# Second expert layer in two parts of two sequences, the first part's routing moved into the end of the attention

## The chip, the cores and the metric

The kernel runs on one core of a Trainium2 chip. The metric is the device time of one execution in microseconds (us). In the rows the engines are PE (TensorE; PEld is its weight load), DVE (VectorE), ACT (ScalarE), POOL (GpSimd) and SP (SyncE); SPq is a transfer issued by SP. TensorE is granted one of two clocks, 1.2 GHz (0.50 in the rows) or 2.4 GHz (1.00).

## What is computed

Two layers over 4 sequences of 512 tokens with 128 features. Layer 0 is a state-space mixer and a mixture of eight experts with a shared one. Layer 1 is a causal attention with 16 heads of 8 features, and then the mixture that the change is about: each token goes to one of eight experts, and the expert's output is weighted with the softmax of the two largest logits and a gate.

```python
logits = flat @ Wr                                  # 2048 tokens x 8 experts
top_vals, top_idx = jax.lax.top_k(logits, 2)
w_top1 = jax.nn.softmax(top_vals, axis=-1)[:, 0]
h = gelu(flat @ W1[top1]); y = h @ W2[top1]         # 128 -> 512 -> 128, the chosen expert alone
x = x + gb * (w_top1 * y)
```

## The kernel before

Each engine runs its own list of instructions in order and waits on semaphores. The order in each list is written out by hand.

**Attention.** The loop `for it in range(-2, 17)` has one step `it` for each group of four heads of a sequence (16 groups), with eight slots `i`. In a slot PE does scores for the group two steps ahead (L1641, into a ring of three PSUM banks), transposed scores (`scores_T`, L1667 and L1672), and in every second slot the product with the values (L1686). DVE takes the maxima (L1221) and ACT the exponentials (L778). POOL cuts the maxima in three bf16 parts (`max_parts`, L522 to L528). PE transposes those (`maxima_T`, L1651), ACT copies them (L817), and SP writes them as rows beside the queries (L364); `scores_T` of the next step waits for these rows. Maxima for group 15 are taken at `it` 13, so DVE has next to nothing from there on.

**Router input.** `x3` of a sequence is ready after its four groups (`attn_out`, L1710 and L1243). `router_input` is a LayerNorm with shift and scale in five steps: statistics and moments on DVE (L387, L392), `ln_rstd` on POOL (L399, L401), normalise (L406), multiply (L539 or L1201), add (L544 or L1206). POOL does the last three for sequences 0 to 2, one half of a sequence's work at each step from `it` 10 on; DVE does them for sequence 3 after the loop.

**Routing, after the attention.** `router` transposes all four sequences (L1367), ACT copies them to SBUF (L831), and PE makes logits for 16 tiles of 128 tokens (L1509). DVE picks the largest (L1088 to L1092), PE counts ranks (L1750, L1751), and DVE turns these into a slot for every token, `posu` (L1275 to L1288). Slots are grouped in blocks of 128, each of one expert: at most 16 + 7 = 23 blocks (`NBLK`). POOL writes the rows of the 16 tiles to their slots in DRAM (`slots_x`, L586), and SP reads all slots back in four groups (L370).

**Blocks.** For each block j, PE transposes it (L1762) and DVE copies the result (L1321); DVE copies the expert's W1 into one of two buffers (L1319); PE makes the hidden layer (L1771, eight records), ACT applies the Gelu (L838), PE makes the output (L1782), and DVE copies it out (L1325). PE issues the transpose of block i+1, the hidden layer of block i and the output of block i-1 in turn. DVE also makes one tile of gate weights a block (L1329). POOL returns each block's rows to their tokens in DRAM (`tokens_y`, L592). After all 23 have landed SP reads four sequences back (L373), `combine` weights and adds them (L413, L415; POOL takes sequence 0, DVE the others), and SP stores them (L381).

## Time and profile before

| what | value |
|---|---|
| median of 3 runs | 581.68 us (579.49 to 581.73) |
| the profiled execution's own time | 577.07 us |
| its span | 575.2 us |
| busy: PE, DVE, ACT, POOL | 452.4, 392.0, 278.1, 271.6 us |
| mean granted clock of PE | 0.889 |

The span runs from the first to the last instruction; 1.87 us of the profiled execution lie around it. Busy time is a sum over stages with different limits. The stretch that the change touches is the last 135 us: the end of the attention (to 467.6 us), routing and row stores (to 511.1 us), blocks (to 558.5 us), and the return (to 575.2 us).

### The profile page before, as it was taken

To read this page: it belongs to the slowest core of one execution; us is meant where nothing else is said; L and a number is where in the kernel's file an instruction comes from. 1 tells how busy PE (TensorE), PEld (TensorE's weight loads), DVE (VectorE), ACT (ScalarE), POOL (GpSimd) and SP (SyncE) were. 2 spreads that over 40 slices of the span, in tenths; PEclk is the share of its full clock that TensorE was granted. 3 is DMA by queue.
4 is the path that set the end of the run, shared out by engine and by line. 5 is a ranking of instruction groups with operands and counts; after the bars stand their busy time and mean duration, and the time that the engine had idled before them with its cause. 6 is when DMAs were issued, how large, how long until landed. Compare 5 with 4: busy or idle time off the path is not lost.

```text
span 575.2 us, 10088 instructions
## 1 busy us (share of the span) xinstructions
PE 452.4 (79%) x3120; PEld 274.4 (48%) x3120; DVE 392.0 (68%) x1264; ACT 278.1 (48%) x518; POOL 271.6 (47%) x392
## 2 busy tenths in 40 slices
PE   3688778987998999994558998999999863059970
PEld 3545456766653444442323434435445343049970
DVE  5789738988655888886679687888898235025533
ACT  1568796653453544441223577678777831013220
POOL 4210038998301786664641047476655502714541
PEclk9988889999799999997775799999999985559995
DMA  8600000000335333310386012222300000141114
GB/s 354 169 1 1 0 2 2 1 2 1 144 148 125 99 106 99 107 62 2 108 208 124 4 31 88 82 86 85 84 5 4 3 0 10 52 123 36 36 38 146
DMA packets 25739, 39.94 MB, mean 69 GB/s; under 512 B 3228, under 2 KB 17756, under 8 KB 25164
## 3 DMA queue, kind: packets, MB, share of 16 engines
q1 hardware_dynamic: 21752, 30.42, 17.8%
q0 software_dynamic: 3936, 8.89, 5.2%
q8 instruction: 26, 0.43, 0.3%
q14 instruction: 25, 0.20, 0.1%
HBM read 27.55 MB, written 11.55 MB: 68 GB/s over the span
## 4 chain that ended last, share of the span: by engine, by line
PE 49%; DVE 18%; POOL 11%; issue 8%; ACT 6%; DMA 6%; SPq 0%; DVEq 0%; POOLq 0%; ACTq 0%
PE ps L1579 5%; PE ps L1581 5%; PE ps L1568 5%; PE ps L1686 4%; PE ps L1599 3%; PE ps L1771 3%; PE ps L1782 3%; POOL slots_x L586 3%; DVE rows L406 3%; PE ps L1391 2%; DVE moe L1221 2%; PE ps L1641 2%; POOL qk_parts L305 2%; DVE st L387 2%; PE ps L1672 2%
## 5 line engine op out<-in xcount | busy, mean ns | idle before, releaser
L1221 DVE CUSTOM_DVE_ANT_0 moe<-ps,const 128x512 bf16<-128x512 f32 (+3 forms) x256 | 110.5, 486 | 9.7 <-PE ps L1641 9.4
L778 ACT ACTIVATE arena<-ps 128x256 f32<-128x256 f32 (+3 forms) x128 | 85.8, 701 | 33.6 <-PE ps L1672 32.9
L476 POOL TENSOR_TENSOR arena<-arena 128x512 f32<-128x512 f32 x32 | 51.7, 1616 | 51.9 <-DVE arena L1139 51.7
L1641 PE MATMUL ps<-arena 48*128 48x128 bf16 (+3 forms) x256 | 56.1, 329 | 10.7 <-DVE arena L1221 4.7
L1672 PE MATMUL ps<-arena 51*128 51x128 bf16 (+3 forms) x256 | 52.2, 307 | 0.0
L1686 PE MATMUL ps<-arena 128*32 128x512 f32 (+3 forms) x512 | 48.4, 450 | 0.9 <-ACT arena L778 0.6
L1667 PE MATMUL ps<-bconst 64*128 64x64 bf16 x512 | 45.6, 195 | 1.2 <-ACT arena L778 0.5
L1641 PEld LDWEIGHTS ps<-arena 48*128 48x128 bf16 x256 | 16.7, 97 | 55.7 <-DVE arena L1221 31.7
L751 ACT ACTIVATE arena<-arena 128x512 f32<-128x512 f32 x32 | 20.2, 630 | 41.9 <-DVE arena L1139 41.6
L838 ACT ACTIVATE arena<-ps 128x512 f32<-128x512 f32 x23 | 13.7, 597 | 55.0 <-PE ps L1771 55.0
L592 POOL DMA_INDIRECT tokens_y<-arena,token_at x23 | 22.1, 960 | 32.5 <-DVE arena L1325 31.3
L950 DVE SCALAR_TENSOR_TENSOR arena<-ps,mixw,arena 128x511 f32<-128x511 f32 (+2 forms) x48 | 33.1, 737 | 5.2 <-ACT arena L643 5.2
L1667 PEld LDWEIGHTS ps<-bconst 64*128 64x128 bf16 x512 | 29.5, 97 | 12.0 <-ACT arena L778 4.5
L1579 PE MATMUL ps<-arena,moe 128*128 128x512 f32 x64 | 32.8, 593 | 1.8 <-DVE arena L1122 1.8
L441 POOL TENSOR_TENSOR arena<-arena 128x256 f32<-128x256 f32 x16 | 12.4, 776 | 44.4 <-DVE arena L933 40.5
L1581 PE MATMUL ps<-arena,moe 128*128 128x512 f32 x64 | 32.7, 592 | 0.0
L1568 PE MATMUL ps<-arena,moe 128*128 128x512 f32 x64 | 32.5, 592 | 0.0
L1130 DVE SCALAR_TENSOR_TENSOR arena<-ps,moe,arena 128x512 f32<-128x512 f32 x32 | 24.0, 751 | 12.3 <-PE ps L1581 12.2
L1762 PE MATMUL ps<-const,arena 128*128 128x128 f32 x23 | 6.5, 293 | 29.1 <-DMA arena<-slots_x 29.1
L1367 PE MATMUL ps<-const,rows 128*128 128x128 f32 x64 | 13.8, 367 | 17.6 <-DVE rows L406 14.9
L1771 PE MATMUL ps<-arena 128*128 128x128 f32 x184 | 26.5, 290 | 0.6 <-DVE arena L1321 0.5
L1139 DVE SCALAR_TENSOR_TENSOR arena<-ps,moe,arena 128x512 f32<-128x512 f32 x32 | 24.0, 751 | 3.5
(239 smaller groups left out, 1113.2 us busy)
## 6 DMA issues: line engine op xcount, KB each, us to landing
arena<-expert_weights SPq DMA_DIRECT2D x32, 256.0 KB, 3.2
arena<-moe_in SPq DMA_DIRECT2D x1, 4100.0 KB, 12.8
qk_parts<-arena SPq DMA_DIRECT2D x24, 128.0 KB, 2.3
qk_parts<-arena POOLq DMA_DIRECT2D x24, 128.0 KB, 2.3
arena<-qk_parts POOLq DMA_DIRECT2D x32, 96.0 KB, 2.5
arena<-qk_parts SPq DMA_DIRECT2D x8, 288.0 KB, 5.6
moe<-moe_in SPq DMA_DIRECT2D x1, 1936.0 KB, 13.8
slots_x<-zeros SPq DMA_DIRECT2D x1, 1518.0 KB, 19.6
```

The source lines that it names most:

```text
L476: pool.tensor_tensor(yacc[:, ts], yacc[:, ts], pr[:, i % 2, :], ALU.add).then_inc(sem("yacc"), 1)
L778: act.activation(pt[:, u % 4, :, 0:n], ps[:, 4 + 2 * k:6 + 2 * k, 0:n], ACT.Exp, scale=ATT_SCALE).then_inc(sem("probs"), 1)
L950: v.scalar_tensor_tensor(out=acc[b % 2][:, c, s:S], in0=ps[:, c, 0:S - s], scalar=w["conv_w"][:, 4 * c + 3 - s:4 * c + 4 - s], in1=acc[b % ...
L1221: v.tensor_tensor_reduce(out=junk[:, done % 2, 0:n], in0=ps[:, k, col:col + n], in1=w["mask"][:, (3 - qt) * P:4 * P], scale=1.0, scalar=3 ...
L1568: pe.matmul(ps[:, 6 + i % 2, :], w["w2"][:, e * D:(e + 1) * D], gT[:, i % 2, :], start=True, stop=True).then_inc(sem("p2_ps"), 1)
L1579: pe.matmul(ps[:, 2 + i % 2, :], w["w1"][:, e * D:(e + 1) * D], xm[:, i % 2, :], start=True, stop=True).then_inc(sem("p1_ps"), 1)
L1581: pe.matmul(ps[:, 4 + i % 2, :], w["w3"][:, e * D:(e + 1) * D], xm[:, i % 2, :], start=True, stop=True).then_inc(sem("p3_ps"), 1)
L1641: mm = pe.matmul(ps[:, k, col:col + n], qaug[lo:lo + KR, b % 2, 2 * g + j // 2, qt * P:(qt + 1) * P], kaug[lo:lo + KR, b % 2, 2 * g + j // ...
L1667: pe.matmul(ps[:, bank, HALF * qh:HALF * (qh + 1)], w["causal"][lo:lo + HALF, qh * P:(qh + 1) * P], w["half"][lo:lo + HALF, :], start=(qh ...
L1672: mm = pe.matmul(ps[:, bank, 0:n], kaug[lo:lo + KM, b % 2, 2 * g + jp, kt * P:(kt + 1) * P], qaug[lo:lo + KM, b % 2, 2 * g + jp, kt * P:S] ...
L1686: mm = pe.matmul(ps[32 * j:32 * j + 32, 3, kt * P:S], va[:, b % 2, kt, 4 * (s % QG) + j, :], pt[:, (2 * m + j // 2) % 4, j % 2, 0:n], star ...
L1771: mm = pe.matmul(ps[:, j % 2, q * P:(q + 1) * P], w1[:, j % 2, q * P:(q + 1) * P], xT[:, j % 2, :], start=True, stop=True)
```

## The change

The 16 tiles are two parts of 8 (sequences 0 and 1, sequences 2 and 3), each with slots and blocks of its own: 8 + 7 = 15 blocks a part, 30 in all.

- POOL's `router_input` of sequences 0 to 2 stands at other steps (it 10 to 14).
- At (13, 7), (14, 1), (14, 4) and (14, 6) PE transposes sequences 0 and 1, makes the logits of 8 tiles, and the ranks, in the ring's banks. ACT copies the two transposes at (14, 0) and (14, 2). DVE does `choose(0)` at (14, 5), and blocks, positions, experts and second best of part 0 at (14, 7).
- POOL then writes part 0's eight tiles (`to_slots(0)`), and only behind them does `ln_rstd` of sequence 3. It returns three blocks of part 0, writes part 1's tiles, and returns the rest; `combine` of sequences 0 and 1 runs on POOL after blocks 4 and 7 of part 1.
- SP reads part 0's slots in three groups once its rows have landed, then part 1's.
- Sequence 2's transpose stands between PE's last two transposes of the attention. After `attn_out(3)` PE has the transpose of sequence 3, two block transposes, part 1's logits, block 0, and on. DVE does the routing of part 1 in pieces between the steps of blocks 0 to 4.
- The last combine is sequence 3 on DVE and sequence 2 on POOL.
- Loads of the constants share one semaphore, and the blocks' buffers lie in areas of the attention that are free by then.

```diff
 HALF = 64
-NBLK = NT + E1 - 1
+PARTS = 2
...
 
+        ROUTER_AT = {(13, 7): ("h4T", 0), (14, 1): ("h4T", 1), (14, 4): ("logits", 0), (14, 6): ("ranks", 0)}
...
+            slots = slots_x.rearrange("(a j p) d -> a p j d", p=P, a=PARTS)
+            for a in range(PARTS):
+                sp.wait_ge(sem(f"scattered{a}"), 16 * PT)
+                if a == 0:
+                    sp.wait_ge(sem("pv"), 4 * QG * (B - 1))
+                for c, js in enumerate(BLOCK_GROUPS):
+                    sp.dma_start(xb[a][:, js, :], slots[a, :, js, :]).then_inc(sem(f"ld_slots{a}{c}"), 16)
+            for a in range(PARTS):
+                sp.wait_ge(sem(f"returned{a}"), 16 * NBLK)
+                for b in (2 * a, 2 * a + 1):
+                    sp.dma_start(yt[:, TPB * b:TPB * (b + 1), :], tokens_y[1 + b * S:1 + (b + 1) * S, :]
+                                 .rearrange("(t p) d -> p t d", p=P)).then_inc(sem(f"ld_y{b}"), 16)
+                for b in ((0, 1), (3, 2))[a]:
+                    if b < 3:
+                        sp.wait_ge(sem("x4_pool"), b + 1)
+                    else:
+                        sp.wait_ge(sem("x4"), 1)
+                    ts = slice(TPB * b, TPB * (b + 1))
...
-                if it >= 10:
-                    b, half = divmod(it - 10, 2)
-                    for step in ((0,), (1, 2))[half]:
-                        router_input(b, step)
-            router_input(2, 1)
-            router_input(2, 2)
+                if it == 10:
+                    router_input(0, 0)
+                    router_input(0, 1)
+                elif it == 11:
+                    router_input(0, 2)
+                    router_input(1, 0)
+                elif it == 12:
+                    router_input(1, 1)
+                    router_input(1, 2)
+                elif it == 13:
+                    router_input(2, 0)
+                elif it == 14:
+                    router_input(2, 1)
+                    router_input(2, 2)
+
+            def to_slots(a):
+
+                pool.wait_ge(sem("posu"), a + 1)
+                pool.wait_ge(sem("h4"), 2 * (a + 1))
+                if a == 0:
+                    pool.wait_ge(sem("slots_clear"), 16)
+                for t in range(PT * a, PT * (a + 1)):
+                    pool.indirect_dma_start(out=slots_x[:, :], out_offset=bass.IndirectOffsetOnAxis(
+                        ap=posu[:, t:t + 1], axis=0), in_=rows[:, t, :], in_offset=None)\
+                        .then_inc(sem(f"scattered{a}"), 16)
+
+            def to_tokens(a, j):
+
+                n = NBLK * a + j
+                pool.wait_ge(sem("pr"), DENSE + n + 1)
+                pool.wait_ge(sem("token_at"), 3 * a + j // 5 + 1)
+                pool.indirect_dma_start(out=tokens_y[:, :], out_offset=bass.IndirectOffsetOnAxis(
+                    ap=token_at[:, n:n + 1], axis=0), in_=xb[a][:, j, 0:D], in_offset=None)\
+                    .then_inc(sem(f"returned{a}"), 16)
+
+            to_slots(0)
             ln_rstd(pool, 4, B - 1)
-
-            pool.wait_ge(sem("posu"), 1)
-            pool.wait_ge(sem("numbers"), 2)
-            pool.wait_ge(sem("h4"), B)
-            pool.wait_ge(sem("slots_clear"), 16)
-            for t in range(NT):
-                pool.indirect_dma_start(out=slots_x[:, :], out_offset=bass.IndirectOffsetOnAxis(
-                    ap=posu[:, t:t + 1], axis=0), in_=rows[:, t, :], in_offset=None).then_inc(sem("scattered"), 16)
-
+            for j in range(RETURNED_FIRST):
+                to_tokens(0, j)
+            to_slots(1)
+            for j in range(RETURNED_FIRST, NBLK):
+                to_tokens(0, j)
             for j in range(NBLK):
-                pool.wait_ge(sem("pr"), DENSE + j + 1)
-                pool.wait_ge(sem("token_at"), j // 6 + 1)
-                pool.indirect_dma_start(out=tokens_y[:, :], out_offset=bass.IndirectOffsetOnAxis(
-                    ap=token_at[:, j:j + 1], axis=0), in_=ys[:, j, :], in_offset=None)\
-                    .then_inc(sem("returned"), 16)
+                to_tokens(1, j)
+                if j in (4, 7):
+                    if j == 4:
+                        pool.wait_ge(sem("gate_weights"), PT)
+                    b = (j - 4) // 3
+                    combine(pool, b, "y_weighted0", "x4_pool", b + 1)
             pool.wait_ge(sem("gate_weights"), NT)
-            combine(pool, 0, "y_weighted0", "x4_0", 1)
+            combine(pool, 2, "y_weighted0", "x4_pool", 3)
 
 
...
+
+            def h4_T(b):
+                k = ring_read(act, "h4T", b)
+                act.activation(hT[:, b * S:(b + 1) * S], ps[:, k, :], ACT.Identity).then_inc(sem("hT"), 1)
+
...
+                    if (it, i) == (15, 4):
+                        top_exp(0)
+
+            weighted(NT - 1)
+            h4_T(2)
+            attention_T(B - 1)
+            h4_T(3)
+            for n in range(0, 6):
+                gelu(n)
+            for n in range(6, PARTS * NBLK):
+                gelu(n)
+            top_exp(1)
 
...
-            for it in range(-2, 17):
+            def slot_step(sem_name, n, ins):
+                ins.then_inc(sem(sem_name), 1)
+                v.wait_ge(sem(sem_name), n)
+
+            TOP, TOP_AT, DIFF, EXP, TOTAL = range(5)
+            LOGITS, HOT, TMP, OTHERS = (lg[:, i] for i in range(4))
+
+            def bcp(a):
+                return a.to_broadcast([P, PT, E1])
+
+            def choose(a):
+
+                k = ring_read(v, "logits", a)
+                slot_step("logits", a + 1, v.tensor_copy(LOGITS, ps[:, k, 0:PT * E1]
+                                                         .rearrange("p (t e) -> p t e", e=E1)))
...
+                slot_step("chosen", a + 1, v.tensor_tensor(HOT, TMP, bcp(lone[:, TOP_AT]), ALU.is_equal))
+
...
+            def expert_blocks(a):
+
+                k = ring_read(v, "ranks", a)
+                slot_step("ranks", a + 1, v.tensor_copy(dp[:, RANK:COUNT + 1].rearrange("p i e t -> p (i e t)"),
+                                                        ps[:, k, 0:2 * PT * E1]))
...
+            def positions(a):
+
...
+                v.tensor_scalar(posu[:, PT * a:PT * (a + 1)], pos[:, :, 0], float(NBLK * P * a - 1), None, ALU.add)\
+                    .then_inc(sem("posu"), 1)
+
+            def block_experts(a):
+
...
+                v.tensor_scalar(expert_at[:, NBLK * a:NBLK * (a + 1)], blk1[:, :, 0], float(E1 - 1), float(HID),
+                                ALU.min, ALU.mult).then_inc(sem("expert_at"), 1)
+
+            def second_best(a):
+
...
+            def top_weight(a):
+
+                v.wait_ge(sem("exp_out"), a + 2)
...
+            for it in range(-2, 16):
                 for i in range(8):
                     if it + 2 < 16:
                         for u in at_slot[i]:
...
+                    if (it, i) == (14, 5):
+                        choose(0)
+                    elif (it, i) == (14, 7):
+                        expert_blocks(0)
+                        positions(0)
+                        block_experts(0)
+                        second_best(0)
+                    elif (it, i) == (15, 7):
+                        top_weight(0)
+
+            def weights_in(n):
+                if n >= 2:
+                    v.wait_ge(sem("p1_ps"), DENSE + n - 1)
+                elif n == 0:
+                    v.wait_ge(sem("pv"), 4 * QG * (B - 1))
+                if n % NBLK == 0:
+                    v.wait_ge(sem("expert_at"), n // NBLK + 1)
+                at_w = v.value_load(expert_at[0:1, n:n + 1], min_val=0, max_val=(E1 - 1) * HID)
+                v.tensor_copy(w1[:, n % 2, :], w["W1"][:, bass.ds(at_w, HID)]).then_inc(sem("w1"), 1)
+
+            def block_in(n):
+                a, j = divmod(n, NBLK)
+                v.wait_ge(sem("xT_ps"), n + 1)
+                v.tensor_copy(xT[:, n % 2, :], ps[:, 2 + n % 2, 0:P]).then_inc(sem("xT"), 1)
+
+            def block_tokens(n):
+                a, j = divmod(n, NBLK)
+                js, ns = slice(j, j + 5), slice(n, n + 5)
+                v.wait_ge(sem(f"ld_slots{a}{j // 5}"), 16)
+                rstep(v.scalar_tensor_tensor(out=spare[:, ns], in0=xb[a][:, js, D], scalar=0.0, in1=w["spare"][:, ns],
+                                             op0=ALU.is_equal, op1=ALU.mult))
+                v.tensor_tensor(token_at[:, ns], spare[:, ns], xb[a][:, js, D], ALU.add).then_inc(sem("token_at"), 1)
+
+            def block_out(n):
+                a, j = divmod(n, NBLK)
+                v.wait_ge(sem("p2_ps"), DENSE + n + 1)
+                v.tensor_copy(xb[a][:, j, 0:D], ps[:, 6 + n % 2, 0:D]).then_inc(sem("pr"), 1)
+
+            def gate_weights(t):
+                if t % PT == 0:
+                    v.wait_ge(sem("wtop"), t // PT + 1)
+                v.tensor_scalar(gw[:, t, :], mod1[:, t // TPB, 3 * D:4 * D], wtop[:, t:t + 1], None, ALU.mult)\
+                    .then_inc(sem("gate_weights"), 1)
+
+            def block_step(i):
+
+                if i % 5 == 0 and i < 2 * NBLK:
+                    block_tokens(i)
+                if i + 1 < 2 * NBLK:
+                    weights_in(i + 1)
+                    if (i + 1) % NBLK > 0:
+                        block_in(i + 1)
+                block_out(i - 1)
+                if (i + 1) % NBLK == 0:
+                    block_out(i)
+                    if i + 1 < 2 * NBLK:
+                        block_in(i + 1)
+
+            o_norm(NT - 1)
+            weights_in(0)
+            weights_in(1)
+            attn_out(B - 1)
+            router_input(B - 1, 0)
+            router_input(B - 1, 1)
+            gate_weights(0)
+            gate_weights(1)
+            gate_weights(2)
+            router_input(B - 1, 2)
+            router_input(B - 1, 3)
+            router_input(B - 1, 4)
+            block_in(0)
+            block_in(1)
+            block_tokens(0)
+            choose(1)
+            weights_in(2)
+            block_in(2)
+            block_out(0)
+            expert_blocks(1)
+            block_step(2)
+            positions(1)
+            block_step(3)
+            block_experts(1)
+            second_best(1)
+            for i in range(4, NBLK):
+                if i < 9:
+                    gate_weights(i - 1)
+                block_step(i)
+            weights_in(NBLK + 1)
+            block_in(NBLK + 1)
+            block_tokens(NBLK)
+            for i in range(NBLK + 1, PARTS * NBLK):
+                block_step(i)
...
                 project_values(b)
-            for it in range(-2, 17):
+            def h4_T(b):
+                k = ring_bank("h4T", b)
+                pe.wait_ge(sem("h4"), b + 1)
+                for i in range(TPB):
+                    mm = pe.transpose(ps[:, k, i * P:(i + 1) * P], xn[:, TPB * b + i, :], ident)
+                mm.then_inc(sem("ring_ps"), 1)
+
+            def logits(a):
+                k = ring_bank("logits", a)
+                pe.wait_ge(sem("ld_moe1"), 16)
+                pe.wait_ge(sem("hT"), 3 * B + 2 * (a + 1))
+                for i in range(PT):
+                    t = PT * a + i
+                    mm = pe.matmul(ps[:, k, E1 * i:E1 * (i + 1)], hT[:, t * P:(t + 1) * P], w["wr"], start=True,
+                                   stop=True)
+                mm.then_inc(sem("ring_ps"), 1)
+
+            def ranks(a):
+                k = ring_bank("ranks", a)
+                pe.wait_ge(sem("chosen"), a + 1)
+                hot = lg[:, 1].rearrange("p t e -> p e t")
+                pe.matmul(ps[:, k, 0:PT * E1], w["tri"], hot, start=True, stop=True)
+                pe.matmul(ps[:, k, PT * E1:2 * PT * E1], ones[:, :], hot, start=True, stop=True)\
+                    .then_inc(sem("ring_ps"), 1)
+
+            router_step = {"h4T": h4_T, "logits": logits, "ranks": ranks}
+
...
-                    elif j == 0:
-                        pe.wait_ge(sem("posu"), 1)
-                    for q in range(4):
-                        mm = pe.matmul(ps[:, 6 + j % 2, 0:D], gs[:, j % 2, q * P:(q + 1) * P],
-                                       w["W2"][:, bass.ds(at_w[j] + q * D, D)], start=(q == 0), stop=(q == 3))
-                    mm.then_inc(sem("p2_ps"), 1)
+            o_T(NT - 1)
+            h4_T(2)
+            a_T(B - 1)
+            attn_out(B - 1)
+            ring_free(pe, 2, RING_MAIN)
+            h4_T(3)
+            block_in(0)
+            block_in(1)
+            logits(1)
+            block_hidden(0)
+            block_step(1)
+            ranks(1)
+            for i in range(2, 8):
+                block_step(i)
+            for i in range(8, NBLK):
+                block_step(i)
+            block_in(NBLK + 1)
+            block_hidden(NBLK)
+            for i in range(NBLK + 1, PARTS * NBLK):
+                block_step(i)
 
 
```

## Rows read from the trace of the kernel before

**Rows 1.** The chain that ended last, in order of time: start us, us, what.

```profile
467.64 0.70 DVE x L1243
...
473.76 1.11 PE ps L1367 x4
474.87 3.23 PE ps L1509 x16
...
485.26 1.14 POOL slots_x L586
...
503.15 0.96 POOL slots_x L586
...
504.41 2.27 DMA slots_x<-rows,posu
506.70 3.29 DMA arena<-slots_x
...
511.12 2.05 PE ps L1771 x8
...
516.44 0.89 PE ps L1771 x8
...
545.50 0.89 PE ps L1771 x8
```

**Rows 2.** Stretches: us; busy (count) of PE, PEld, DVE, ACT, POOL; clock; DMA share, GB/s.

```profile
448.00:455.00 7.00, 6.24 (x88) 2.33 (x88) 1.05 (x6) 6.25 (x11) 5.94 (x11) 1.00 0.01 4
307.00:314.00 7.00, 6.11 (x27) 1.56 (x27) 6.15 (x29) 2.88 (x4) 0.66 (x4) 0.50 0.77 128
511.00:515.70 4.70, 4.58 (x21) 4.61 (x22) 1.62 (x6) 1.17 (x2) 0.00 (x0) 0.50 0.54 148
515.70:558.00 42.30, 42.02 (x370) 41.19 (x368) 22.36 (x83) 12.57 (x22) 20.44 (x22) 1.00 0.11 34
```

**Rows 3.** Instructions in order of time, around step 13 and 14 of the attention.

```profile
432.04 1.04 POOL L401 TENSOR_TENSOR rs<-rs,neghalf 128x4 f32<-128x4 f32 x1
433.19 3.14 POOL L406 TENSOR_SCALAR rows<-x,mv,rs 128x128 f32<-128x128 f32 x4
444.85 0.37 DVE L392 BATCH_NORM_AGGREGATE mv<-st 128x2 f32<-128x6 f32 x4
448.57 0.21 POOL L522 CAST arena<-arena 128x16 bf16<-128x16 f32 x1 [5.79 <-DVE arena L1221]
449.82 0.39 PE L1651 MATMUL ps<-bconst,arena 128*12 128x128 bf16 x4
450.78 0.66 PE L1695 MATMUL ps<-const,mod 128*128 128x128 f32 x4
455.05 0.23 PE L1667 MATMUL ps<-bconst 64*128 64x64 bf16 x4 [0.45 <-DMA arena<-arena]
468.73 1.06 PE L1509 MATMUL ps<-arena,hT 128*128 128x8 f32 x8 [0.25 <-ACT hT L831]
```

**Rows 4.** Groups of instructions: count, busy us, mean ns, idle before them and its releaser.

```profile
L592 POOL DMA_INDIRECT tokens_y<-arena,token_at x23 | 22.1, 960 | 32.5 <-DVE arena L1325 31.3 <-DVE token_at L1311 0.9 <-issue 0.3
L1319 DVE COPY arena<-arena 128x512 f32 x22 | 9.4, 427 | 10.5 <-issue 7.1 <-PE ps L1771 3.4
L920 DVE SCALAR_TENSOR_TENSOR arena<-arena 128x64 f32<-128x64 f32 x6 | 1.3, 216 | 0.0
```

**Rows 5.** Instructions in order of time: one block's wait on DVE, and the combines.

```profile
520.16 0.29 DVE L1325 COPY arena<-ps 128x128 f32<-128x128 f32 x1 [0.41 <-PE ps L1782]
...
564.24 1.26 POOL L413 TENSOR_TENSOR arena<-arena 128x512 f32<-128x512 f32 x1 [4.29 <-DMA arena<-tokens_y]
565.58 1.59 POOL L415 TENSOR_TENSOR x<-x,arena 128x512 f32<-128x512 f32 x1
566.08 1.63 DVE L415 TENSOR_TENSOR x<-x,arena 128x512 f32<-128x512 f32 x1
569.68 0.69 DVE L415 TENSOR_TENSOR x<-x,arena 128x512 f32<-128x512 f32 x1
```

360 lines of the change are left out of this document (166 added, 194 removed).

## Prediction

> **What bounds the kernel now.** I read the page's slices first: they show which engine is busy when. PE is nearly always busy until 470 us, then goes quiet at the low clock, and fills the slices again from 510 us. The chain of waits in order of time then says what the quiet stretch is. The reader should see four links in it [rows 1]: sequence 3's router input, from `x3` at 467.64 us to the transpose at 473.76; logits, choice and ranks until the first row store at 485.26; sixteen row stores, the last at 504.41, with landing and reading back until 510; and from 511.12 blocks on PE. From the last router input to the first hidden layer pass 511.12 - 473.76 = 37.4 us in which PE has 5 us of work. Blocks then cost (545.50 - 516.44) / 15 = 1.94 us each [rows 1]. That stage is PE's: 42.02 us busy of 42.30 [rows 2]. The instructions in order of time around steps 13 and 14 [rows 3] say how much room the attention has for routing work: DVE has plenty, PE little, 6.24 busy of 7.00 us [rows 2].
>
> **The attention with part 0's routing in it.** I walked PE's list through steps 13 and 14 with the new items. Added to PE: two sets of four transposes at 0.66 us like L1695's, logits of 8 tiles at twice the 0.96 us to be read between starts behind the 1.06 us of L1509's eight records (a tile is two records) [rows 3], ranks at about 0.6 us: 3.85 us. New waits: POOL's `router_input(2, 0)` now stands ahead of `max_parts(15)`. It can start when the moments are there, 444.85 + 0.37, and takes 1.04 us for the power, some 0.4 for the step ahead of it and the gaps, and 3.14 for the normalise: 449.9 instead of the 448.57 at which `max_parts(15)` started. So its four steps end some 1.3 us later, and PE's `maxima_T`, which began at 449.82, right behind them, is late by as much [rows 3]. PE is late itself by the two transposes (1.3 us), so this costs only 0.2 to 0.3. `ranks(0)` waits for `choose(0)`: six DVE steps of 128x64 at 0.21 us [rows 4] plus 0.05 of waiting are 1.7 us, behind which PE has 1.1 us of work: 0.6 lost. Against that the old stalls are used up: 0.45 at 455.05 for the rows [rows 3] and some 0.7 more in waits for ACT. 3.85 + 0.9 - 1.15 = 3.6 us. Bounds: 1.5 if half of PE's work fits between ACT's exponentials, 5 if nothing is absorbed. ACT's two copies fit in its idle time. DVE's work at (14, 7), some 4.5 us, stands ahead of `o_norm(14)`, which nobody needs before the last copy of step 15. The transpose of sequence 2 takes PE's wait for DVE before the last transposes, at no price. `weights_in(0)` and `(1)`, 2 us, lie in DVE's 2.6 us before `attn_out(3)`.
>
> **Part 0's row stores.** `posu(0)` is ready 3.2 us after ranks, near 460.6. Eight stores at (504.41 - 485.26) / 15 = 1.277 us [rows 1] end near 471.1. Sequence 3's `ln_rstd`, queued behind them on POOL, is ready near 473.2 (x3 at 467.6 + 3.6, and 2 us of statistics): cover of 2 us. Without that cover each us goes to the end. The rows land and are read back 2.27 + 3.29 us after the last store's start, at 475.5; PE asks for them after h4 of sequence 3, at 473.76 + 3.6 = 477.4. So the first hidden layer waits for neither; PE has the transpose (1.11), two block transposes (1.0) and half of the old logits' tiles, which take 3.23 us because the clock is low (the 3.23 us of L1509's sixteen records are eight tiles [rows 1]): 5.3 us. **Saved between h4(3) and the first hidden layer: 37.4 - 5.3 = 32.0 us.** Bounds: 30 to 33.
>
> **Blocks.** Seven more at 1.94: +13.6 us. Routing of part 1 puts some 20 small steps, 6 us, on DVE between steps 0 and 4, where a block leaves DVE 0.4 us of wait [rows 5] beside its unhidden issue time. Following both lists, hidden layer 3 waits for the W1 copy behind ranks, 4 and 5 for the copies behind `positions` and `second_best`; the fifth block starts 13.4 us after the first where it was 10.85 before: +2.5 (bounds 0 to 5). At the border of the parts PE makes output 14 with nothing between, then needs a transpose, its copy on DVE and a second transpose: +1.3 (0.6 to 2). The two combines on POOL run beside DVE's copies. The combines of before show what that does: DVE's second operation took 1.63 us beside POOL's 1.59 and 0.69 alone [rows 5]. A block's slack takes most of it: +1.0 (0 to 4). Sum +18.4.
>
> Part 1's rows: `posu(1)` near 491.3; POOL returns block 2 and starts the eight stores near 494.6; they are read back at 510. Block 15 is wanted near 516.7. So they are hidden with 6.7 us of cover. POOL then has twelve returns behind them (15.3 us) and catches up with the blocks near 520.
>
> DVE's W1 copy does 512 columns in 0.43 us, while POOL's returns beside such copies took 0.960 us, just as a store beside an idle DVE, 0.96 [rows 1, 4]. The Trainium skill (SBUF — State Buffer, Who interferes with whom) says that a copy in a two-port mode locks POOL's descriptor writing out for its whole length. By the row eight stores in the blocks cost what they cost before; by the rule each may wait for one copy of 0.43, 3.4 us in all, which would use half of the 6.7 us of cover, and the sum would stay. The trace so far speaks against that rule here.
>
> **The return.** Sequences 0 and 1 are combined and stored during the blocks. At the end one combine stays on each of DVE and POOL, where DVE had three: 569.68 + 0.69 = 570.37 [rows 5] becomes the end of the first pair, near 567.7, and two stores instead of four follow it. -2.2 us (-1.5 to -3).
>
> **Sum.** +3.6 - 32.0 + 18.4 - 2.2 = -12.2 us: the profiled execution's 577.07 us would be 564.9. It lay 4.6 us under the median 581.68; against the median the same difference gives 569.5 us. The zero fill of the slots (30 blocks, not 23) is issued in the first stage with hundreds of us to land, at nothing; constants under one semaphore have landed long before their reader.
>
> **Rivals.**
> - *The clock stays low over the blocks (slower).* The first two blocks of before ran at 0.50 for 4.7 us, then at 1.00 [rows 2], 2.05 us for a hidden layer against 0.89 [rows 1]. Low, a block costs 1.8 to 1.9 us more. In the stretch from 307 to 314 us PE was busy 6.11 of 7.00 us and stayed at 0.50 [rows 2]. DVE's routing leaves PE gaps of 1 to 1.5 us in steps 2 to 5. If the clock rises only after some 7 blocks beyond the first, the gain is gone (12.2 / 1.85 = 6.6); through all of part 0 it would be 569.5 + 15 x 1.85 = 597. Against it: at the low clock PE's 3.7 us a block outlast DVE's, so the gaps close. Chance 0.07. A milder form, 3 blocks at the low clock: 575, chance 0.1.
> - *Part 1's rows are late.* DVE's positions come later or stores are slowed, by more than the 6.7 us; at 10 us late the sum loses 3.3: 573. Chance 0.06.
> - *Combines lock DVE out.* The same section of the skill calls the port an exclusive lock. Worked from rows: two combines hold POOL 2 x (1.26 + 1.59) = 5.7 us [rows 5], less four blocks' slack of 0.4: 4.1 instead of 1.0, so 572.6. The combine row (1.63 against 0.69) goes its way in part. Chance 0.08.
> - *Part 0's stores hold up sequence 3.* If `posu(0)` comes 5 us later than I think, or the attention slips less than 2 us, `ln_rstd` waits 2 to 3 us: 572. For it: the chain of DVE steps is long. Against: a shorter attention gives back what the wait takes. Chance 0.08.
> - *No effect*: it would need stalls of 12 us more, from several of these. Chance 0.03.
>
> The forecast itself: 0.58.
>
> **Range and chances.** The forecast's own terms give -18 (all low bounds, half of them at once unlikely) to -4 us; rivals but the first lie at 572 to 575; runs of one kernel here spread by 2 us and the profiled one lay 4.6 below. So 562 to 577. Faster by over 0.5% (under 578.8 us; 0.5% is about what a measurement tells from no change here) 0.88, within 0.5% 0.05, slower 0.07.
>
> **What the profile after would show.** The first hidden layer near 482 to 483 us, at most two stalls of PE over 0.5 us in steps 14 and 15, and the end of step 15 some 3.6 us later. POOL's eight stores inside step 15 and before `ln_rstd`. No wait of PE for `slots_x` beyond 1 us at block 0 or 15. PE's clock back at 1.00 by 484 us. Steps 2 to 5 at 2.2 to 3 us, all others at 1.9. The last block copied out near 548 us. The prediction is wrong if the first hidden layer starts after 487 us, if PE waits at block 15, or if the clock is low after 490 us.

## The result, and the profile after

The changed kernel takes 572.28 us, median of 4 runs (570.89 to 572.88), against 580.59 (578.03 to 581.73) for the kernel before, run beside it: ratio 0.9883, 95% interval 0.9854 to 0.9913. Forecast were 569.5 us (562 to 577), faster. The profiled execution after has a span of 570.2 us and a time of 572.55.

The page's slices of the kernel after, PE and its granted clock, each slice 14.3 us:

```profile
PE   3688678988897999995657998998989983899960
PEclk9988799999799999999775599999999987899995
```

Of the quiet stretch of the kernel before, 37 us between router input and first hidden layer, one slice with a 3 is left, the 34th (470 to 485 us). To see where the difference went I cut both executions at the same instructions (the first exponential of an attention step, the end of `x3(3)`, the first gelu, the last output's copy, the end), in us:

| | start to step 13 | step 13 | step 14 | step 15 to x3(3) | to first gelu | blocks | return |
|---|---|---|---|---|---|---|---|
| before | 440.08 | 8.19 | 7.12 | 12.95 | 44.88 | 45.27 | 16.77 |
| after | 442.71 | 8.77 | 10.97 | 13.32 | 13.16 | 63.88 | 17.43 |
| difference | +2.63 | +0.58 | +3.85 | +0.37 | -31.72 | +18.61 | +0.66 |

The sum is -5.0, the difference of the spans; the medians differ by 8.3. In the first column the change touches little (order of POOL's `router_input` from step 10 on, the wait for constants, the zero fill), and it varies from execution to execution: the kernel of experiment 1 and the identical one of experiment 9 have 442.61 and 440.00 there, and the two profiles of kernels in one part (before, experiment 2) 440.08 and 445.32. So only the later columns are compared; they sum to -7.6.

**Steps 14 and 15**, the instructions in order of time of the kernel after; they answer to [rows 3]:

```profile
449.41 3.14 POOL L437 TENSOR_SCALAR rows<-x,mv,rs 128x128 f32<-128x128 f32 x4
...
452.50 0.21 POOL L553 CAST arena<-arena 128x16 bf16<-128x16 f32 x1
...
453.65 0.39 PE L1808 MATMUL ps<-bconst,arena 128*12 128x128 bf16 x4 [0.24 <-POOL arena L559]
...
455.52 1.95 PE L1889 MATMUL ps<-arena,hT 128*128 128x8 f32 x16
...
459.17 0.45 PE L1897 MATMUL ps<-mixw,const 128*128 128x64 f32 x2 [0.42 <-DVE mixw L1349]
...
460.57 1.51 PE L1843 MATMUL ps<-arena 128*32 128x384 f32 x8
...
463.55 1.14 POOL L626 DMA_INDIRECT slots_x<-rows,posu  x1 [7.37 <-DVE posu L1376]
```

POOL's `max_parts(15)` stands behind the normalise and PE waits 0.24 for it; logits take 1.95; ranks wait 0.42. What the forecast lacked is the last PE row: 1.51 us for what took 0.85 a step before. The stretches (busy us and instructions of PE, PEld, DVE, ACT, POOL, then granted clock, DMA share, GB/s) show why:

```profile
457.00:459.00 2.00, 1.75 (x25) 0.82 (x24) 1.32 (x6) 1.02 (x2) 0.00 (x0) 1.00 0.01 3
459.00:460.00 1.00, 0.83 (x8) 0.74 (x10) 0.02 (x1) 0.82 (x1) 0.00 (x0) 0.72 0.00 0
460.00:462.00 2.00, 2.00 (x15) 0.31 (x14) 1.65 (x8) 1.02 (x1) 0.00 (x0) 0.50 0.00 0
...
475.00:480.00 5.00, 0.04 (x1) 0.00 (x0) 3.61 (x16) 0.00 (x0) 1.55 (x2) 0.65 0.77 203
480.00:485.00 5.00, 3.08 (x14) 2.74 (x14) 2.13 (x6) 1.88 (x2) 0.00 (x0) 0.50 0.00 0
485.00:490.00 5.00, 5.00 (x25) 5.00 (x25) 1.34 (x6) 0.60 (x1) 0.00 (x0) 0.50 0.00 0
490.00:500.00 10.00, 8.26 (x68) 7.54 (x67) 6.76 (x29) 2.39 (x4) 3.52 (x4) 0.99 0.07 23
```

The clock falls to 1.2 GHz near 459.5, right behind PE's one wait of 0.42 us, and again when PE waits for the last layer norm, where it stays until 490. That the short wait brings the first fall about looks plausible, but other traces speak against it. In six of the ten profiles with the same code in step 14 (the changed kernel and experiments 1, 3, 4, 6 to 10 and 12) the clock fell ahead of ranks, with no wait over 0.3 us before it in the step, and `ranks` then waited for nothing. Experiment 12 is one of them:

```profile
455.00:460.00 5.00, 5.00 (x48) 3.10 (x45) 1.89 (x8) 2.67 (x5) 1.15 (x1) 0.76 0.01 2
460.00:465.00 5.00, 5.00 (x49) 1.61 (x48) 3.83 (x18) 2.38 (x5) 0.91 (x1) 0.56 0.01 3
```

PE is busy all of the ten us there. In the kernel before it was busy for only 2.96 of the 5 us from 460 to 465, in step 15, and the clock stayed at 1.00. So what brings the clock down in step 14 stays open.

**From x3(3) to the first hidden layer**, in order of time:

```profile
477.19 0.50 POOL L430 TENSOR_SCALAR rs<-mv 128x4 f32<-128x4 f32 x1 [3.64 <-DVE mv L423]
...
481.57 1.09 PE L1880 MATMUL ps<-const,rows 128*128 128x128 f32 x4 [6.52 <-DVE rows L1286]
...
483.43 3.56 PE L1889 MATMUL ps<-arena,hT 128*128 128x8 f32 x16 [0.35 <-ACT hT L873]
...
486.84 2.06 PE L1950 MATMUL ps<-arena 128*128 128x128 f32 x8
```

POOL has been idle for 3.64 us when the last moments come: part 0's stores are hidden, with that cover. From the transpose to the first hidden layer it is 5.3 us, where before it was 37.4 [rows 1].

**The blocks**: hidden layers that wait for DVE during part 1's routing, and then a combine beside a copy. The last two rows here answer to [rows 5]:

```profile
494.75 1.16 PE L1950 MATMUL ps<-arena 128*128 128x128 f32 x8 [0.81 <-DVE arena L1435]
...
497.81 1.16 PE L1950 MATMUL ps<-arena 128*128 128x128 f32 x8 [0.90 <-DVE arena L1435]
...
535.18 1.27 POOL L446 TENSOR_TENSOR x<-x,arena 128x512 f32<-128x512 f32 x1
535.20 1.54 DVE L1430 COPY arena<-arena 128x512 f32 x1 [0.44 <-issue]
```

DVE's copy, issued 0.02 us behind POOL's addition, takes 1.54 us instead of the 0.43 of [rows 4]: it ends 0.29 after POOL. The Trainium skill (SBUF — State Buffer, Who interferes with whom) says of a DVE copy in a two-port mode and POOL that whichever issues first holds the shared ports for its whole instruction; the trace agrees here. For row stores beside copies the trace is kinder: of sixteen the shortest is 0.957 us, the median 0.962, the longest, the first of them, 1.137 (in experiments 3 and 4 up to 1.20). At the border of the parts PE doesn't wait for part 1's rows; its wait there is 0.36 us, for DVE's copy.

**The return.** The instructions that close each engine's list all carry one line, L71 (L69 in the kernel before). One of them is a DRAIN. The rows give count, shortest, median and longest in ns, then first and last start in us; they follow POOL's last addition, after:

```profile
560.00 1.59 POOL L446 TENSOR_TENSOR x<-x,arena 128x512 f32<-128x512 f32 x1
...
L71 POOLq DRAIN  x1: 10048/10048/10048, 560.0 to 560.0; - x1
L71 DVEq DRAIN  x1: 1672/1672/1672, 560.5 to 560.5; - x1
L71 SPq COMPARE_BRANCH  x1: 38/38/38, 565.1 to 565.1; - x1
L71 SPq EVENT_SEMAPHORE  x1: 17/17/17, 570.2 to 570.2; - x1
```

The last output has landed when SP branches, at 565.1. POOL's drain ends at 570.0, 8.4 us behind the end of its last addition, and the kernel ends at 570.2. The same rows before:

```profile
L69 POOLq DRAIN  x1: 9475/9475/9475, 565.5 to 565.5; - x1
...
L69 SPq COMPARE_BRANCH  x1: 33/33/33, 572.6 to 572.6; - x1
```

There too the drain outlasts the stores: it ends at 575.0, 7.8 us behind the addition at 565.58 [rows 5], and SP is done at 572.6. The return that the change was to shorten by 2.2 us is 0.7 longer.

### The profile page after: what moved, and what is told of

Read it like the earlier page. It is cut to its first block, busy times and chain, and to the rows that moved or that the text cites. A ratio compares the mean times of both kernels' runs of the same rounds, so it can differ in the third digit from the quotient of the medians.

```text
span 570.2 us, 10516 instructions
## 1 busy us (share of the span) xinstructions
PE 467.0 (82%) x3243; PEld 288.0 (51%) x3243; DVE 403.6 (71%) x1312; ACT 283.6 (50%) x527; POOL 284.0 (50%) x403
## 4 chain that ended last, share of the span: by engine, by line
PE 51%; DVE 18%; POOL 10%; issue 7%; ACT 7%; DMA 5%; DVEq 0%; SPq 0%; POOLq 0%; ACTq 0%
PE ps L1739 5%; PE ps L1741 5%; PE ps L1728 5%; PE ps L1843 4%; PE ps L1950 3%; PE ps L1757 3%; PE ps L1959 3%; DVE rows L437 3%; PE ps L1566 2%; PE ps L1798 2%; POOL qk_parts L332 2%; PE ps L1829 2%; DVE st L418 2%; DVE moe L1301 2%; PE ps L1654 2%
## 5 line engine op out<-in xcount | busy, mean ns | idle before, releaser
L635 POOL DMA_INDIRECT tokens_y<-arena,token_at x30 | 29.2, 973 | 30.8 <-DVE arena L1448 25.9
L883 ACT ACTIVATE arena<-ps 128x512 f32<-128x512 f32 x30 | 17.9, 598 | 48.7 <-PE ps L1950 48.7
L1950 PE MATMUL ps<-arena 128*128 128x128 f32 x240 | 34.2, 288 | 4.1 <-DVE arena L1435 4.0
L1824 PEld LDWEIGHTS ps<-bconst 64*128 64x128 bf16 x512 | 29.2, 97 | 11.2 <-issue 2.4
L472 POOL TENSOR_TENSOR arena<-arena 128x256 f32<-128x256 f32 x16 | 12.4, 775 | 45.2 <-DVE arena L1013 41.3
L1950 PEld LDWEIGHTS ps<-arena 128*128 128x128 f32 x240 | 30.7, 200 | 6.1 <-DVE arena L1435 6.0
L1210 DVE SCALAR_TENSOR_TENSOR arena<-ps,moe,arena 128x512 f32<-128x512 f32 x32 | 24.1, 752 | 12.1 <-PE ps L1741 12.1
L1959 PE MATMUL ps<-arena 128*128 x240 | 31.7, 276 | 0.0
L1959 PEld LDWEIGHTS ps<-arena 128*128 128x128 f32 x240 | 29.2, 192 | 0.1
## 6 DMA issues: line engine op xcount, KB each, us to landing
arena<-moe_in SPq DMA_DIRECT2D x1, 4100.0 KB, 12.8
```

Of the source, the lines that this page charges most:

```text
L1824: pe.matmul(ps[:, bank, HALF * qh:HALF * (qh + 1)], w["causal"][lo:lo + HALF, qh * P:(qh + 1) * P], w["half"][lo:lo + HALF, :], start=(qh ...
L1950: mm = pe.matmul(ps[:, 4 + n % 2, q * P:(q + 1) * P], w1[:, n % 2, q * P:(q + 1) * P], xT[:, n % 2, :], start=True, stop=True)
L1959: mm = pe.matmul(ps[:, 6 + n % 2, 0:D], gs[:, n % 2, q * P:(q + 1) * P], w["W2"][:, bass.ds(at_w[n] + q * D, D)], start=(q == 0), stop=(q ...
```

## The experiments

Twelve runs, on four chips; the kernel before is run beside each. "dve_end" is the kernel of experiment 1. The stages are those of the table above (steps 14 and 15 with x3, to the first gelu, blocks, return). The same code varies a little: with ranks in place, step 14 takes 10.8 to 11.0 us where the clock falls in it for 3.4 us, and 11.2 to 11.7 where it falls for 6.8, so a difference under 1 us in that column says nothing of an edit.

| | median us (runs) | ratio to before | step 14 | 15, x3 | to gelu | blocks | return |
|---|---|---|---|---|---|---|---|
| 1 dve_end | 566.19 (6) | 0.9784 [0.9749, 0.9819] | 11.69 | 13.63 | 13.16 | 64.56 | 11.16 |
| 2 before, same edit | 575.88 (12) | 0.9932 [0.9899, 0.9964] | 7.12 | 12.94 | 45.14 | 45.43 | 13.63 |
| 3 stores behind | 584.67 (4) | 1.0099 [1.0066, 1.0132] | 11.48 | 13.90 | 23.75 | 64.55 | 18.33 |
| 4 eight returns first | 580.00 (10) | 1.0017 [0.9983, 1.0051] | 11.54 | 13.79 | 13.17 | 71.12 | 17.55 |
| 5 ranks late | 581.85 (12) | 1.0054 [1.0030, 1.0078] | 10.13 | 19.19 | 13.17 | 76.92 | 11.41 |
| 6 all combines on DVE | 586.32 (6) | 1.0112 [1.0082, 1.0142] | 10.83 | 23.82 | 13.17 | 74.97 | 10.93 |
| 7 PE kept busy | 589.75 (6) | 1.0175 [1.0136, 1.0215] | 11.46 | 23.81 | 14.40 | 76.87 | 11.21 |
| 8 routing left out | 589.42 (4) | 1.0152 [1.0106, 1.0197] | 11.21 | 23.81 | 13.17 | 75.89 | 11.07 |
| 9 dve_end again | 568.24 (5) | 0.9823 [0.9800, 0.9847] | 11.46 | 13.95 | 13.17 | 64.73 | 11.25 |
| 10 the sixth again | 563.56 (4) | 0.9758 [0.9724, 0.9793] | 10.83 | 13.54 | 13.16 | 62.31 | 11.02 |
| 11 10 with ranks late | 566.00 (4) | 0.9792 [0.9740, 0.9844] | 9.12 | 13.51 | 13.16 | 63.20 | 11.13 |
| 12 10 with PE kept busy | 564.77 (4) | 0.9760 [0.9719, 0.9801] | 11.53 | 13.81 | 12.37 | 62.81 | 11.06 |

**1. The last combine of POOL moved to DVE.** Sequences 0 and 1 stay on POOL. SP stores sequence 2 ahead of 3, as DVE makes them.

```diff
-            pool.wait_ge(sem("gate_weights"), NT)
-            combine(pool, 2, "y_weighted0", "x4_pool", 3)
...
+            combine(v, 2, "y_weighted", "x4", 1)
+            combine(v, 3, "y_weighted", "x4", 2)
```

> Against the changed kernel: the last combine of sequence 2 goes from POOL to DVE, which then does sequences 2 and 3 one after the other. Theory (POOL's drain sets the end): in the changed kernel all engines waited for POOL's drain, which ended 8.5 us after POOL's last tensor operation (561.59), at 570.05, while the last store had landed at 565. Without that combine POOL's drain starts after its last return (554.3) and ends near 563, so the end is the landing of the last store. DVE's two combines without POOL beside them take 4 x 0.68 = 2.7 us, as long as its one beside POOL. The span ends 4 to 5 us earlier: about 567.6 us as a median, against 572.3. Rival (the wait at the end has another cause, PE's or a fixed one): same time within 1 us, near 572.

It gave 566.19 us, 6 less than the changed kernel, all of it in the return (17.43 to 11.16). The last line's instructions:

```profile
L71 POOLq DRAIN  x1: 9828/9828/9828, 554.5 to 554.5; - x1
...
L71 SPq COMPARE_BRANCH  x1: 38/38/38, 565.2 to 565.2; - x1
...
L71 SPq EVENT_SEMAPHORE  x1: 17/17/17, 565.5 to 565.5; - x1
```

POOL's drain starts 5.5 us sooner and is over at 564.3, before the last output lands. Of the 6.3 us in the return 4.7 are what the drain had stood beyond SP's branch. The other 1.6 are stores that land sooner: DVE's four operations take 0.69 us each now, where its two beside POOL's took 1.03 and 1.63.

**2. The same in the kernel before**, whose sequence 0 went to POOL at the end.

```diff
-            pool.wait_ge(sem("gate_weights"), NT)
-            combine(pool, 0, "y_weighted0", "x4_0", 1)
...
-            for b in range(1, B):
+            for b in range(B):
```

> Against the kernel before: the combine of sequence 0 goes from POOL to DVE, which does all four. Theory (POOL's drain sets the end here too): POOL's last tensor operation ended at 567.17 and its drain at 575.0, while the last store landed at 572.6. Four combines on DVE alone take 4 x 1.35 = 5.4 us from 564.3, so the last store is issued near 569.8 and lands near 572.3: 2 to 3 us less than before, about 578 us as a median. Rival (POOL's drain does not matter): DVE has one combine more and loses POOL's help, 0 to +1 us against before.

The return fell from 16.77 to 13.63 us and the ratio is 0.9932. POOL's drain, over at 573.4 with SP's branch at 577.4, no longer counts. It was a cost of the kernel before too, a smaller one: 2.3 of the 3.1 us; the other 0.9 are stores that land sooner.

**3. Part 0's stores behind sequence 3's `ln_rstd`** on POOL, the step of that router input which POOL does.

```diff
+            ln_rstd(pool, 4, B - 1)
             to_slots(0)
-            ln_rstd(pool, 4, B - 1)
```

> Against the changed kernel: on POOL the ln_rstd of sequence 3 stands ahead of the eight row stores of part 0 instead of behind them, so the stores are no longer beside the end of the attention. Theory (the gain is the row stores beside the chain of the last sequence): the first store starts at 478.9 instead of 463.6, the rows are read back near 494.6 instead of 480, and PE's first block transpose, which was at 482.5, waits for them: +12 us, about 584 us, slower than before the change. Rival (another link, DVE's router input or the low clock, would take most of it anyway): +5 us or less.

584.67 us, 12.4 more than the changed kernel and more than the kernel before; the stretch to the first gelu grew by 10.6 us. So the whole gain hangs on the place of these eight stores in POOL's queue.

**4. Eight outputs returned ahead of part 1's stores, not three.**

```diff
-        RETURNED_FIRST = 3
+        RETURNED_FIRST = 8
```

> Against the changed kernel: POOL returns eight blocks of part 0 before it writes part 1's rows, not three. Theory (part 1's rows are hidden with 6.5 us of cover in the changed kernel: read back near 514, wanted at 520.5): the stores start near 508 instead of 499.5, the rows are read back near 523.6 and PE waits 3 us for them at block 15: +3 us, about 575. Rival (PE waits for something else at the border of the parts, or the cover is larger): no difference over 1 us.

580.0 us, 7.7 more, where 3 were expected. In order of time and in stretches:

```profile
517.72 0.96 POOL L626 DMA_INDIRECT slots_x<-rows,posu  x1 [0.30 <-issue]
...
523.38 0.69 PE L1939 MATMUL ps<-const,arena 128*128 128x128 f32 x2 [4.54 <-DMA arena<-slots_x]
...
524.24 2.08 PE L1950 MATMUL ps<-arena 128*128 128x128 f32 x8 [0.17 <-DVE arena L1435]
```

```profile
515.00:520.00 5.00, 3.84 (x34) 3.58 (x32) 1.82 (x6) 1.19 (x2) 3.91 (x4) 1.00 0.17 55
520.00:525.00 5.00, 1.45 (x5) 1.05 (x6) 0.30 (x2) 0.00 (x0) 3.83 (x4) 0.77 0.84 239
525.00:530.00 5.00, 5.00 (x28) 5.00 (x27) 1.84 (x7) 1.19 (x2) 1.91 (x2) 0.54 0.18 59
```

Counted from the first gelu, the last store comes 30.85 us later instead of 19.43, and PE waits 4.54 us for the rows: 11.42 - 4.54 leaves a cover of 6.9 us in the changed kernel. The wait has a second price: the clock falls to 1.2 GHz at its end and the next blocks cost some 2.4 us more.

**5 to 8. Four edits of dve_end on one chip**: ranks of part 0 and the choice of experts later (5), all combines on DVE at the end (6), ten matmuls that nobody reads in PE's wait for the last layer norm (7), and part 1's last twelve routing steps on DVE left out, so that rows of part 1 go to wrong places (8).

```diff
-        ROUTER_AT = {..., (14, 6): ("ranks", 0)}
+        ROUTER_AT = {..., (15, 0): ("ranks", 0)}
...
-                    if (it, i) == (15, 4):
+                    if (it, i) == (15, 6):
```

> Against e1_dve_end: the ranks of part 0 are at (15, 0) instead of (14, 6), and the Exp of part 0's weights at (15, 6) instead of (15, 4). Theory (in step 14 PE's wait of 0.42 us for choose(0) comes with a fall of the clock to 0.50 from 459.4 to 462.7 us, in which the product with the values took 1.51 us instead of 0.85): without the wait the clock stays at 1.00, and the stretch from the start of step 14 to x3 of sequence 3 becomes 1.5 us shorter (23.9 us in the changed kernel, 22.4 then). part 0's stores start 1.5 us later, which their cover of 3.6 us holds. Median about 564.7. Rival (the length of step 14 is the sum of PE's added work, the clock falls anyway): the same stretch within 0.3 us.

```diff
-                if j in (4, 7):
-                    ...
-                    combine(pool, b, "y_weighted0", "x4_pool", b + 1)
...
-            combine(v, 2, "y_weighted", "x4", 1)
-            combine(v, 3, "y_weighted", "x4", 2)
+            for b in range(B):
+                combine(v, b, "y_weighted", "x4", b + 1)
```

> Against e1_dve_end: the combines of sequences 0 and 1 leave POOL (and the blocks) and go to DVE while it waits for the last return; SP reads sequences 2 and 3 before it stores 0 and 1. Theory (POOL's combines hold up DVE's W1 copies, one of which took 1.54 us instead of 0.43, and PE waited 0.56 and 0.88 us): blocks 15 to 29 are 1.4 us shorter, and DVE's 2.7 us fit between its last gate weights and the landing of the last return. 1.4 us less, about 564.8. Rival (the two stores beside the last read slow it down, or the copies would have been late anyway): same or up to 1 us more.

```diff
             ring_free(pe, 2, RING_MAIN)
+            for i in range(10):
+                pe.matmul(ps[:, 7, :], ident, w["mask"], start=True, stop=True)
             h4_T(3)
```

> Against e1_dve_end: PE does ten matrix products of 128x512 that nobody reads (5.9 us at 0.59) after attn_out(3), where it waited 6.5 us for sequence 3's router input. Theory (the low clock from some 477 to 490 us costs: transpose 1.1 instead of 0.66, logits 3.56 instead of 1.95, the first two hidden layers 1.9 and 1.7 instead of 0.9 each): the clock stays at 1.00 and block 2's hidden layer starts 3.8 us earlier after x3 than in the changed kernel (16.8 us there, 13.0 then). About 562.5 us. Rival (the products end too late and push the transpose back, or DVE's and ACT's steps set that stretch): less than 1 us gained.

```diff
+                if a == 0:
-                rstep(v.tensor_tensor(nblk[:, 2, :], nblk[:, 1, :], nblk[:, 0, :], ALU.subtract))
+                    rstep(v.tensor_tensor(nblk[:, 2, :], nblk[:, 1, :], nblk[:, 0, :], ALU.subtract))
...
```

> Against e1_dve_end. It leaves out 12 of DVE's small steps of part 1's routing between the first blocks (counts to blocks, positions, the experts of the blocks), so that part 1's rows go to the slots of part 0's tokens and its blocks to part 0's experts. Theory (DVE's routing steps are what stretches the first blocks, +2.8 us between the starts of block 0 and 5 against before): those 3.3 us of DVE's time come out of the path nearly whole, 13.7 us from hidden layer 0 to 5 become 11 or less; about 563.5 us. Rival (ranks on PE and the low clock stretch them): 1 us or less gained.

All four came out 15 to 24 us above dve_end, while the kernel before was as always (579.62). None of my theories had that. The time was lost at two places common to the four: step 15 (19.2 to 23.8 us instead of 13.6) and four blocks of part 0 (blocks 75 to 77 us instead of 64.6). Both are where POOL stores rows. Experiment 6, in order of time:

```profile
513.94 1.15 PE L1950 MATMUL ps<-arena 128*128 x8 [1.15 <-issue]
...
517.52 0.29 DVE L1438 COPY arena<-ps 128x128 f32<-128x128 f32 x1 [5.94 <-remote]
...
519.00 2.07 PE L1941 MATMUL ps<-arena 128*128 128x128 f32 x8 [3.80 <-DVE arena L1425]
...
523.25 1.08 ACT L873 ACTIVATE arena<-ps 128x512 f32<-128x512 f32 x2 [9.45 <-remote]
```

PE's matmul ends at 515.1 and DVE, which waits for nothing else, starts 2.4 us later; PE's next ends at 521.1 and ACT starts 2.2 later. "Remote" says that the profile finds no releaser at that moment. Over the whole trace, starts of ACT or DVE over 1.2 us behind the matmul that they wait for number 4 to 6 past 430 us in each of these four kernels; the kernels before and after and experiments 1 to 4 have none there. POOL's own issues stay at 0.96. The trace's semaphore events put PE's update 0.02 us ahead of an ordinary start, and as close to 13 of these 18 late ones. So in these the update comes late, and the engine that waits starts at once. The ends of matmuls are modelled, so whether PE's last results or its signal is late, the trace doesn't tell.

Of their own questions these four answer one. In experiment 8 the third and fourth interval between gelus lie ahead of the disturbance: 1.92 and 1.90 us, where dve_end has 2.97 and 3.07. So part 1's routing costs 2.2 us in these two. The second interval is 0.9 longer (3.26 instead of 2.37), as it is in experiment 11 (3.12): in both the clock comes back more than 3 us behind the first gelu, in dve_end 1.6 us behind it.

**9 and 10. Two of these kernels again, unchanged, side by side on another chip**: dve_end and the one with all combines on DVE.

> The kernel of the first experiment once more, unchanged, because four kernels built on it came out 15 to 25 us above it, and in all four ACT and DVE start 1.2 to 5.7 us after the end of the matmul that they wait for, at four to seven places beside POOL's row stores, which this kernel's trace showed nowhere (none over 1.2 us). Theory A, the delay belongs to the chip that the four ran on and to POOL's stores lying beside compute: this kernel behaves as the combines kernel beside it in this call does; on a chip with the delay it gives 581 to 590 us with such waits at 465-476 and 510-525, on one without it 564 to 570. Theory B, the delay comes from the edits of the four: this kernel gives 566 us and has no such wait, while the one beside it gives 586.

> The kernel with all combines on DVE once more, unchanged, in one call with the kernel that it is built on. Theory A, the delay belongs to the chip: both have it or neither; where neither has it, this one gives 562 to 570 us (the same as the kernel it is built on, within 4 us). Theory B, the delay comes from the edits: 584 to 588 us here, with 4 to 7 starts over 1.2 us late, and 566 us for the other.

568.24 and 563.56 us, and no such late start past 430 us in either. The sixth kernel took 586.32 us on one chip and 563.56 on another, each time beside a kernel before at 578 to 580. The same stretch in both, experiment 10 and then experiment 6:

```profile
515.00:525.00 10.00, 9.57 (x82) 9.02 (x81) 4.65 (x17) 2.99 (x5) 7.07 (x8) 1.00 0.14 47
```

```profile
515.00:525.00 10.00, 3.29 (x15) 2.80 (x14) 2.28 (x8) 1.08 (x2) 5.75 (x6) 0.58 0.51 143
```

So the delay isn't made by the edits; theory A holds as far as that. That POOL's stores to the slots beside compute bring it about on that chip rests on place alone. The late starts lie between the first of eight such stores and 6 us behind the last, while the rows land and SP reads them back, so the landing and the reading back are rivals that no run separates. The returns, which POOL issues the same way beside all other blocks, have none, and the kernel before, which stores all rows while the other engines wait, showed no loss there. What delays them wasn't found, and the changed kernel itself wasn't run on that chip.

Experiment 10 is the fastest kernel. Against 9, on the same chip, it gains 2.4 us in the blocks and 0.2 in the return: about what the two combines on POOL cost. The 1.0 us that it gains in steps 14 and 15 isn't the edit's, which changes nothing there: the clock was low for 3.4 us in one and 6.8 in the other.

**11. Ranks late, on the kernel of experiment 10.** The edit is that of experiment 5.

> The ranks-late experiment again, on the kernel with all combines on DVE (its ratio to before 0.9758), to see it without the late starts. The two rank matmuls of part 0 go from place (14, 6) to (15, 0), the expert choice from (15, 4) to (15, 6). Theory A, the placement of these steps made step 14 take 3.7 us longer, by PE waiting in its order for POOL and DVE: the stage from the start of step 13 to the end of x3(3) shortens by 1.5 to 3 us, and part 0's stores start some 3 us later and still end before they are waited for; ratio 0.970 to 0.975. Theory B, the time in step 14 and 15 is that of the added PE work itself and of the clock that falls to 0.50 after PE's short waits near 457: moved, it costs the same one step later; the stage stays within 1 us and the ratio within 0.973 to 0.979. If the late starts come in this call, the ratio is near 1.00 and tells nothing of either.

Step 14 took 9.12 us instead of 10.83, and the clock there stayed up. Experiment 11, then 10:

```profile
455.00:460.00 5.00, 5.00 (x59) 2.84 (x58) 1.89 (x8) 3.44 (x6) 1.24 (x1) 1.00 0.01 2
460.00:465.00 5.00, 4.71 (x69) 2.33 (x68) 3.48 (x16) 3.75 (x8) 0.49 (x1) 1.00 0.01 3
```

```profile
455.00:460.00 5.00, 4.58 (x46) 1.86 (x47) 3.03 (x14) 2.86 (x3) 0.00 (x0) 0.79 0.00 1
460.00:465.00 5.00, 4.61 (x74) 2.00 (x70) 2.78 (x14) 3.19 (x8) 2.88 (x3) 0.87 0.10 30
```

The stage shortened by 1.7 us, which is theory A's size, but 0.9 came back: the clock, low from later on, also stayed low longer in the first blocks. The ratio, 0.9792, is no better than 0.9758 and outside theory A's range. That the clock stayed up need not be the edit's doing: with the same ranks-late edit experiment 5 saw it fall in step 14 for 3.4 us, ahead of any late start, and took 10.13 us. Taken from these three, moving ranks is worth some 0.7 us in step 14 (10.83 to 10.13), and the fall costs some 1.0 (10.13 to 9.12).

**12. PE kept busy, on the kernel of experiment 10.** The edit is that of experiment 7.

> The kept-busy experiment again, on the kernel with all combines on DVE: ten 128x512 fp32 matmuls that nobody reads, after attn_out(3), where PE waits 6.5 us for the last layer norm. Theory A, that wait is why the granted clock is 0.50 from 477 to 490, where the prediction had it back by 484: filled, the clock stays at 1.00, the ten take 6 us inside the wait, the router of part 1 takes 2.0 us instead of 3.6 and the first two blocks' matmuls half their time; hidden 0 starts 1 to 2 us earlier and total is 3 to 5 us lower, ratio 0.967 to 0.971. Theory B, the clock falls anyway, before the wait, from the thin work in steps 15 and after it: the ten take 8 to 10 us and push what follows back by 2 to 4 us; ratio 0.977 to 0.983. If the late starts come in this call, the ratio is near 1.01 and tells nothing of either.

```profile
475.92 8.75 PE L1973 MATMUL ps<-const 128*128 128x512 f32 x20
```

```profile
475.00:480.00 5.00, 5.00 (x18) 2.83 (x19) 3.03 (x14) 0.00 (x0) 1.55 (x2) 1.00 0.72 197
480.00:485.00 5.00, 5.00 (x16) 2.34 (x15) 2.40 (x6) 0.00 (x0) 0.00 (x0) 1.00 0.02 6
485.00:490.00 5.00, 4.44 (x32) 4.23 (x31) 2.06 (x10) 2.48 (x3) 0.00 (x0) 0.83 0.01 3
```

PE's wait is the reason for the low clock from 477 on: filled, the clock stayed at 1.00 past 485, and was low for 3.4 us later. But the ten took 8.75 us and not 6, so the transpose ended 1.4 us later; from there to the first gelu it took 2.2 less, and the blocks behind 0.5 more. The sum is -0.3 us, the ratio the same, 0.9760. Theory A is right about the cause, and neither is right about the price.

## Why the prediction was right, and where it wasn't

*The main term* held: -32.0 us forecast between h4(3), sequence 3's router input, and the first hidden layer; 5.3 us are left there, as forecast. Its condition, part 0's stores ahead of sequence 3's router input and out of its way, had 3.6 us of cover instead of 2, since the attention slipped more. Experiment 3 shows that the gain is lost without it.

*The attention*: +3.6 forecast, 0.58 + 3.85 + 0.37 = 4.8 measured, inside the bounds of 1.5 to 5. The waits were as walked through (0.24 for POOL, 0.42 instead of 0.6 for DVE). The mis-sized part is the clock, which the forecast let stand at 1.00: it was low for 3.4 us in step 14. In experiment 11, where it stayed up, the three terms are 0.58 + 2.00 + 0.56 = 3.1 us. Why the clock fell is open: in six profiles it did so with no wait of PE over 0.3 us ahead of it in that step, and with ranks elsewhere it fell once and once not.

*The blocks*: +18.4 forecast, +18.6 measured. The terms were each off a little, and that they add up so closely is luck. From the gelu's intervals: the first five take 12.76 us instead of 9.86, +2.9 for routing (2.5 forecast); the border of the parts takes 3.67 + 1.34 instead of 3.80, +1.2 (1.3); two intervals beside combines are 0.8 longer each, +1.7 (1.0). By experiments 9 and 10 the combines cost 2.2 to 2.4 us. The rival "combines lock DVE out" had the mechanism, with 4.1 us too high a price. The rest, 12.8, is seven blocks at 1.8 (13.6 forecast).

*Part 1's rows* were hidden with 6.9 us of cover by experiment 4 (6.7 forecast). The 3.4 us that the prediction weighed for copies that hold up the stores did not come: the median store took 0.962 us, as its rows had it.

*The return* is the step that failed in sign: "the end of the first pair, near 567.7" was taken for what sets the end, -2.2 us. The last combine on DVE did end 2.6 us sooner, counted from the last output's copy, and SP's branch came 1.8 us sooner, but neither sets the end. POOL's drain, which no row of the forecast had, set it in both kernels. POOL's own last addition ends 8.7 and 8.8 us behind the last output's copy, and the drain is over 7.8 and 8.4 us behind the addition: that is the 0.7 us. With POOL done earlier (experiment 1) the return shrinks by 6.3 us.

*The low clock*: it was to be back by 484 us and was back at 490. Of the 6 us, 4 are the later start of the whole stage (2.63 ahead of step 13 and 1.2 more in the attention); the other 2 are not explained. The rival "clock stays low over the blocks" did not come: from the third hidden layer at 491.88 it is high.

Of the forecast's three signs of being wrong, PE's wait for rows at block 15 did not come. The first hidden layer at 486.84 us is just short of the second (487). The clock came back just past the third (490): it is 0.50 up to 490 and 0.99 over 490 to 500. The stages show that the shift ahead of step 13 is the largest part of both.

Forecast sum -12.2, measured -8.3 by medians and -7.6 by the stages from step 13 on. The attention is 1.2 over and the return 2.9 over, 4.1 together; the shift of 2.63 ahead of step 13 is in one profiled pair only. The bounds that the forecast gave for its terms add up to -20.3 to -1.9, not to the -18 to -4 that it named; the measured difference lies in either.

## What to carry to other kernels

A step moved beside other work is worth only as much as its place in a queue: name the cover in us, then test it by moving the step behind its neighbour. At the end of a kernel look at every engine's drain, not only at the last store: give the last work to an engine whose drain is short. And a long gap of PE (4.5 us in experiment 4, 6.5 in the changed kernel) is paid twice where the clock falls with it, though filling the gap cost about what it saved in experiment 12.
